# Learning-rate projection as 32-column blocks over token quarters, ahead of the value projections

## What is computed

```
XQ = rope(heads(xn @ q_w.T)); XK = rope(heads(xn @ k_w.T)); XV = heads(xn @ v_w.T)
ttt_lr = sigmoid(einsum('bnkc,hdc->bhnkd', Xc, lr_w) + lr_b)
eta = token_idx * ttt_lr / HD          # used in every step of the scan
out = scan(step, (W1, b1), chunks of (XQ, XK, XV, eta))
y = ln(out) @ o_w.T
```

## Time and profile before

| what | us |
|---|---|
| median of 3 runs | 676.73 (676.66 to 681.01) |
| the profiled execution | 677.36 |
| its span in the trace | 675.3 |
| what lies around the span | 2.06 |

### The profile page before, as it was taken

The page is one execution under the profiler, slowest core; times in us unless marked ns, Lnnn a source line. Parts: engine busy times, 40 slices in busy tenths (PEclk is TensorE's granted clock), DMA queues, the critical chain, the costliest instruction groups (busy, mean ns, idle before and its releaser), DMA issues. The chain is left out here.

```text
span 675.3 us, 30660 instructions
## 1 busy us (share of the span) xinstructions
PE 523.9 (78%) x12150; PEld 365.4 (54%) x12150; DVE 474.2 (70%) x1484; ACT 365.1 (54%) x1172; POOL 339.4 (50%) x595
## 2 busy tenths in 40 slices
PE   0399999997477777777777777777776499859997
PEld 0143333444466777766777677677775244445552
DVE  6456776753668888888888888888897267528331
ACT  0424443223556666666666766666665576544432
POOL 0368888775334544544555445455543656421223
PEclk9999999997555555555555555555555699969999
DMA  9101111113900000000000000000000700000113
GB/s 348 48 8 40 39 39 32 31 31 79 203 6 2 0 0 0 0 0 0 0 0 0 0 0 0 0 0 0 0 3 3 282 1 0 1 1 1 65 73 114
DMA packets 9849, 24.54 MB, mean 36 GB/s; under 512 B 1845, under 2 KB 2510, under 8 KB 9550
## 3 DMA queue, kind: packets, MB, share of 16 engines
q1 hardware_dynamic: 9806, 24.01, 11.5%
HBM read 11.42 MB, written 4.19 MB: 23 GB/s over the span
## 5 line engine op out<-in xcount | busy, mean ns | idle before, releaser
L762 PE MATMUL PS<-work 32*32 32x32 f32 x4064 | 84.5, 238 | 60.0 <-DVE work L911 52.7
L762 PEld LDWEIGHTS PS<-work 32*32 32x32 f32 x4064 | 80.4, 152 | 70.2 <-issue 66.7
L751 PE MATMUL PS<-work 64*32 64x64 f32 x2048 | 69.6, 310 | 24.1 <-ACT work L1002 20.5
L500 PE MATMUL PS<-X,work 128*128 (+3 forms) x160 | 72.4, 599 | 6.4 <-ACT X L640 6.3
L751 PEld LDWEIGHTS PS<-work 64*32 64x32 f32 x2048 | 55.7, 163 | 31.2 <-issue 29.8
L774 PE MATMUL PS<-work 32*64 32x32 f32 x2016 | 68.4, 292 | 1.1 <-issue 1.1
L966 POOL TENSOR_TENSOR work<-work 128x128 f32<-128x128 f32 x64 | 25.5, 399 | 80.7 <-DVE work L911 77.2
L774 PEld LDWEIGHTS PS<-work 32*64 32x64 f32 x2016 | 59.7, 216 | 5.3 <-issue 1.3
L958 POOL TENSOR_TENSOR work<-work,mask 128x256 f32<-128x256 f32 x64 | 46.7, 730 | 13.6 <-ACT work L1034 7.3
L942 POOL TENSOR_TENSOR work<-KP,cst 128x256 f32<-128x256 f32 x64 | 39.2, 612 | 26.5 <-DVE work L870 21.5
L500 PEld LDWEIGHTS PS<-X,work 128*128 128x128 f32 (+1 forms) x160 | 26.1, 171 | 47.7 <-issue 47.2
(11 more groups left out here) (145 smaller groups left out, 1301.2 us busy)
## 6 DMA issues: line engine op xcount, KB each, us to landing
X<-in_x SPq DMA_DIRECT2D x4, 1024.0 KB, 8.0
TK<-KP SPq DMA_DIRECT2D x64, 64.0 KB, 1.9
X<-QP SPq DMA_DIRECT2D x8, 512.0 KB, 9.0
TK<-in_x SPq DMA_DIRECT2D x4, 1024.0 KB, 8.9
out<-TK SPq DMA_DIRECT2D x16, 256.0 KB, 2.2
work<-in_rope SPq DMA_DIRECT2D x2, 512.0 KB, 9.7
cst<-in_consts SPq DMA_DIRECT2D x1, 289.0 KB, 4.8
work<-in_wk SPq DMA_DIRECT2D x1, 256.0 KB, 11.1
```

The costliest lines, as they stand in the source:

```text
L500: mm = nc.tensor.matmul(o, lhs(j), xt(i, j), start=(j == 0), stop=(j == J - 1))
L751: mm = nc.tensor.matmul(PS[HD * a:HD * a + HD, ZB[p], b * ZW:b * ZW + ZW], KT2[p][r:r + 64, k * B + b, :, :].rearrange("p e t -> p (e t)") ...
L762: mm = nc.tensor.matmul(PS[HD * a:HD * a + HD, bank, b * width:b * width + HD], AM[p][HD * a:HD * a + HD, b, part, :, :].rearrange("p e t ...
```

## The change

The rates are computed with 32 weight columns instead of 8 (24 are zeros, set by a memset on POOL; SP's load of wl waits for it). Four matmuls for each channel half take 128 tokens each and write them to the partitions 0-31, 32-63, 64-95 and 96-127 of bank 2, columns 0 to 127. They stand after the four rotary projections, ahead of the widening and the value projections. lr_out becomes a copy of 128 partitions x 128 columns, ahead of the two v_out; it goes to lrt for block 0 and to the first 128 columns of the block i-1 of X, which is done with. PE's hardware loop over the blocks becomes straight code for all of them, and ACT's body 0 is taken out of its loop. At the end there are eight 128 x 128 transposes into the banks 1 and 2 in place of the 32, and two sigmoids of 128 columns in place of one of 256.

```diff
--- before.py
+++ after.py
@@ -226,12 +226,13 @@
         sd = carve(P)
         kc, ksw = carve(2, BLK), carve(2, BLK)
         wkv = carve(J, 2 * C)
-        wl = carve(J, NH)
+        wl = carve(J, HD)
         sum_x, sum_sq = carve(BLK), carve(BLK)
         wvw = wsm
         lrt = sb("lrt", [P, 8 * B * NH])
         s_k0 = sem("s_k0")
         s_pick = sem("pick_rows")
+        s_wl0 = sem("wl_zero")
         s_w, s_rt, s_sp2 = sem("s_w"), sem("ropetab"), sem("spread_table")
 
         FIRST = CONST_AT["spread"][0]
@@ -246,7 +247,8 @@
             sp.dma_start(wkv[:, :, 0:C], wk).then_inc(s_w, 16)
             sp.dma_start(wkv[:, :, C:2 * C], wq).then_inc(s_w, 16)
             sp.dma_start(wvw[:, :, :], wv).then_inc(s_w, 16)
-            sp.dma_start(wl, wlr).then_inc(s_w, 16)
+            sp.wait_ge(s_wl0, 1)
+            sp.dma_start(wl[:, :, 0:NH], wlr).then_inc(s_w, 16)
             sp.dma_start(cosT, rope[:, 0, :]).then_inc(s_rt, 16)
             sp.dma_start(sinT, rope[:, 1, :]).then_inc(s_rt, 16)
             sp.dma_start(cst[:, FIRST:], consts[:, FIRST:]).then_inc(s_sp2, 16)
@@ -298,6 +300,7 @@
                 pool.memset(eps5, EPS_GN).then_inc(s_k0, 1)
                 pool.memset(eps6, EPS_IN).then_inc(s_k0, 1)
                 pool.memset(one, 1.0).then_inc(s_k0, 1)
+                pool.memset(wl, 0.0).then_inc(s_wl0, 1)
                 pool.memset(pick[:, :, :], 0.0).then_inc(s_pick, 1)
                 pool.wait_ge(s_pick, 1)
                 for g in range(4):
@@ -450,6 +453,12 @@
                 sem(n) for n in ("proj", "kc", "ksw", "ksin", "rope", "tt", "lr", "kperm", "ttf", "lr_tr", "sig",
                                  "lr_spread", "lr_h"))
             NPJ = 7
+
+            def rate_rows(i):
+
+                if isinstance(i, int) and i == 0:
+                    return lrt[:, 0:P]
+                return X[:, 0, ds((i - 1) * BLK, P)]
 
             @block.sync
             def _(sp):
@@ -478,26 +487,26 @@
                 def proj(i, m, first):
                     if m < 2 * J:
                         lhs = lambda j: wkv[:, j, m * P:(m + 1) * P]
-                    elif m < 3 * J:
+                    else:
                         lhs = lambda j: wvw[:, j, (m - 2 * J) * P:(m - 2 * J + 1) * P]
-                    else:
-                        lhs = lambda j: wl[:, j, :]
-                    if m == NPJ - 1:
-                        first_tile = value(pe, i * (2 * J) + 1)
-                        pe.wait_ge(s_w, 64)
-                        pe.wait_ge(s_ksw, first_tile)
-                        o = PS[0:NH, 2, :]
-                    else:
-                        o = PS[:, 2 + m, :]
-                        if not first:
-                            if m < 2 * J:
-                                pe.wait_ge(s_ksw, (i - 1) * (2 * J) + m + 1)
-                            else:
-                                pe.wait_ge(s_tt, (i - 1) * J + m - 2 * J + 1)
-                            if m == 0:
-                                pe.wait_ge(s_lr, i + 0)
+                    if not first:
+                        if m < 2 * J:
+                            pe.wait_ge(s_ksw, (i - 1) * (2 * J) + m + 1)
+                        else:
+                            pe.wait_ge(s_tt, (i - 1) * J + m - 2 * J + 1)
+                        if m == 0:
+                            pe.wait_ge(s_lr, i + 0)
                     for j in range(J):
-                        mm = nc.tensor.matmul(o, lhs(j), xt(i, j), start=(j == 0), stop=(j == J - 1))
+                        mm = nc.tensor.matmul(PS[:, 2 + m, :], lhs(j), xt(i, j), start=(j == 0), stop=(j == J - 1))
+                    mm.then_inc(s_proj, 1)
+
+                def rates(i):
+                    pe.wait_ge(s_ksw, value(pe, i * (2 * J) + 1))
+                    for j in range(J):
+                        for g in range(4):
+                            mm = nc.tensor.matmul(PS[HD * g:HD * g + HD, 2, 0:P], wl[:, j, :],
+                                                  xt(i, j)[:, g * P:(g + 1) * P], start=(j == 0),
+                                                  stop=(j == J - 1), skip_group_check=True)
                     mm.then_inc(s_proj, 1)
 
                 def body(i, first):
@@ -506,9 +515,12 @@
                     if has(i, 1):
                         pe_var(pe, i + 1, False)
                     pe.wait_ge(q1["xn"], i * J + J)
-                    for m in range(NPJ):
-                        if m == 2 * J and has(i, 1):
-                            pe_widen(pe, i + 1, False)
+                    for m in range(2 * J):
+                        proj(i, m, first)
+                    rates(i)
+                    if has(i, 1):
+                        pe_widen(pe, i + 1, False)
+                    for m in range(2 * J, 3 * J):
                         proj(i, m, first)
 
                 pe_mean(pe, 0, True)
@@ -516,21 +528,16 @@
                 pe_var(pe, 0, True)
                 pe_widen(pe, 0, True)
                 body(0, True)
-                with pe.Fori(1, NBLK - 2) as i:
+                for i in range(1, NBLK):
                     body(i, False)
-                body(NBLK - 2, False)
-                body(NBLK - 1, False)
 
                 pe.wait_ge(s_lr, NBLK)
                 pe.wait_ge(q1["xh"], NBLK * J)
-                for b in range(B):
-                    for s in range(8):
-                        tr = nc.tensor.transpose(PS[:, 1, (s * B + b) * NH:(s * B + b + 1) * NH],
-                                                 X[0:NH, 0, b * N + s * P:b * N + (s + 1) * P],
-                                                 ident[0:NH, 0:NH])
+                for i in range(NBLK):
+                    tr = nc.tensor.transpose(PS[:, 1 + i // 4, (i % 4) * P:(i % 4 + 1) * P], rate_rows(i), ident)
                 tr.then_inc(s_tr, 1)
 
-                pe.wait_ge(s_sig, 1)
+                pe.wait_ge(s_sig, 2)
                 pe.wait_ge(s_sp2, 16)
                 pe.wait_ge(q1["xc"], NBLK * J)
                 for n in range(8):
@@ -631,14 +638,14 @@
             @block.scalar
             def _(act):
                 def v_out(i, j):
-                    act.wait_ge(s_proj, i * NPJ + 2 * J + j + 1)
+                    act.wait_ge(s_proj, i * NPJ + 2 * J + j + 2)
                     nc.scalar.activation(TT[:, j, ds(i * BLK, BLK)], PS[:, 2 + 2 * J + j, :], ACT.Identity,
                                          scale=neg_g[:, j:j + 1], bias=bbg[:, j:j + 1]).then_inc(s_tt, 1)
 
                 def lr_out(i):
-                    act.wait_ge(s_proj, i * NPJ + NPJ)
-                    nc.scalar.activation(X[0:NH, 0, ds(i * BLK, BLK)], PS[0:NH, 2, :], ACT.Identity,
-                                         bias=pcol("lr_b", rows=NH)).then_inc(s_lr, 1)
+                    act.wait_ge(s_proj, i * NPJ + 2 * J + 1)
+                    nc.scalar.activation(rate_rows(i), PS[:, 2, 0:P], ACT.Identity, bias=pcol("lr_b")
+                                         ).then_inc(s_lr, 1)
 
                 def body(i):
                     if has(i, 1):
@@ -649,9 +656,9 @@
                         act_square(act, i + 2, False)
                     if has(i, 1):
                         act_affine(act, i + 1)
+                    lr_out(i)
                     for j in range(J):
                         v_out(i, j)
-                    lr_out(i)
 
                 act.wait_ge(s_sp, 2 * J)
                 act_a(act, 0)
@@ -661,12 +668,17 @@
                 act_sd(act, 0, True)
                 act_square(act, 1, False)
                 act_affine(act, 0)
-                with act.Fori(0, NBLK - 3) as i:
+                body(0)
+                with act.Fori(1, NBLK - 3) as i:
                     body(i)
                 for i in range(NBLK - 3, NBLK):
                     body(i)
                 act.wait_ge(s_tr, 1)
-                nc.scalar.activation(lrt[:, :], PS[:, 1, 0:8 * B * NH], ACT.Sigmoid).then_inc(s_sig, 1)
+                for k in range(2):
+                    nc.scalar.activation(
+                        lrt.rearrange("p (s b h) -> p b s h", s=8, b=B)[:, 2 * k:2 * k + 2, :, :],
+                        PS[:, 1 + k, :].rearrange("p (b s h) -> p b s h", b=2, s=8)[:, :, :, 0:NH], ACT.Sigmoid
+                    ).then_inc(s_sig, 1)
```

## The result

| | before | after |
|---|---|---|
| median of 8 runs each, us | 678.0 (676.66 to 681.5) | 671.45 (669.89 to 673.74) |
| profiled execution, us | 677.36 | 672.6 |
| span, us | 675.3 | 670.4 |

The ratio of the times is 0.9897, with a 95% interval of 0.9869 to 0.9924: 1.0% faster, 6.55 us by the medians. The forecast was 669.8 in a range of 666.0 to 674.5, with 0.50 for faster by over 1% and 0.47 for within 1%; the interval has 0.99 inside, so the runs don't decide between these two. The median lies 1.65 us above the forecast; the gain is 6.55 where 6.9 was forecast, and the rest of the distance is the kernel before, whose median over eight runs is 678.0 and not the 676.73 from which I started.

A forecast was written before the change was run, and what follows sets the result against it. The prediction took a ring of POOL, DVE and ACT, without PE, to bound the projections. Blocks gave 1.28 + 1.00 + 1.23 + 1.54 = 5.05 us, with the tail 6.9: 677.36 - 6.9 = 670.5, median 669.8, range 666.0 to 674.5.

The forecast's parts named there:

- The ring without PE: Projections: a closed chain of waits through POOL, DVE and ACT sets the 15.42 us from one token block to the next.
- lr_out, 0.32 a turn: Projections: ACT's smaller copy of the rates saves 0.32 us per block in four blocks, 1.28 us.
- The rates, 0.43 to 0.60 on PE: Projections: sixteen passes take 0.43 us, 0.60 with changes of shape, replacing 1.88; by itself this buys nothing in the middle.
- PE's earlier start: Projections: PE starts 1.64 us earlier against the ring; blocks 5, 6 and 7 gain 1.00, 1.23 and 1.54 us.
- The tail: After the last projection block, v_out to spread: the spread starts at 153.6 instead of 160.48, 6.9 us earlier.
- The straight code: PE's unrolled loop moves its instruction-fetch stop in the scan: taken as zero, between 3.38 us gained and 13.1 lost.
- PE as the bound: Rival 1, projections: PE binds, four turns give 5.3 us instead of 1.28, total 665.8 us; chance 0.10.
- the sizes wrong: Rival 2: column groups run serially (1.71 us), ACT's copy gets no shorter; some 3.7 us gained, 673 us; chance 0.20.
- the third: Rival 3, early scan: PE runs out of code until eight transfers finish, at worst 13.1 us lost, 682.9; chance 0.05.
- The Trainium skill's rule on instruction fetching: Instructions come in 16 KiB blocks, fetched ahead, mostly hidden; by it straight code costs nothing and 669.8 us stays.

The follow-up runs named there:

- the ring cut: Changed kernel with ACT's scale of a block (act_a) issued one block sooner, in ACT's idle time: 667.53 us, ratio 0.9794 against the kernel before.
- the place alone: Changed kernel with the old rates (8 columns, 512 tokens, large copy, 32 transposes) in the new place: 672.54 us, ratio 0.9888 against the kernel before.
- the hold-back: Eight transfers X<-QP let go one by one from the scan's ninth chunk: changed kernel 664.56 us (0.9767), kernel before 672.88 us (0.9887).
- The form alone: Changed kernel with rates and their copy put back last on PE and ACT, new shapes kept: 678.04 us, ratio 0.9986 against the kernel before.

## Why the prediction was right, point by point

- **The ring without PE bounds the turn.** Right, and shown by both signs: 0.86 us more on PE changes nothing, 1.7 more by a slow clock neither, 0.25 more on ACT lengthens each turn by 0.25, and with the ring cut at act_a the turn falls to POOL's 14.04 (14.09 follows from the prediction's 15.42 less POOL's 1.33).
- **lr_out, 0.32 a turn.** Right in the ordinary turn, 15.42 to 15.10, and by its size: in its new place with the old size (the place alone) it gives nothing in the turn. That POOL reaches block 4 1.33 us earlier, where 1.28 was forecast for four turns, is partly luck. By its product for the second key tile the four turns gave 0.36, 0.12, 0.33 and 0.33, 1.14 in all, since the second has the 0.2 of ACT described above; 0.19 were there before the first of them.
- **The rates, 0.43 to 0.60 on PE.** Right: 0.64 with the last pass's tail, 0.57 from start to start. It wasn't a term of the sum in the middle, and three times as much of it cost nothing.
- **PE's earlier start.** Right in size: 1.33 and 1.62 between the last blocks, 1.23 and 1.54 forecast. I had written about 1.6 us for PE's wait for lr_out; it is 0.96, and another 0.64 lies ahead of the variance, where PE waits for DVE's scale to have read bank 1. The sum was right, the place of a part wasn't, and no term of the time hung on it.
- **The tail.** The spread at 153.49, forecast 153.6. That the scan starts 6.97 us earlier is good to a few tenths: the two kernels with the hold-back, whose projections are the same code, have 6.7 between them.
- **The straight code.** Taken as zero with bounds of -3.38 and +13.1: -1.8 when done alone, at most +0.46 in the profile of after, where 0.4 remain with the stops gone. That zero was so near is luck: the stops to the 7th chunk are worth 8.1 us in the kernels before and after and 4.9 in the place alone. The reason that I gave, that what was asked for comes when the queues empty, holds by half: in the trace one block came at 170.2, with the transfers still running, and the next at 179.0, as they ended.
- **What I left out.** The forecast of the profiled execution was 670.5 and it took 672.6. Of the 2.1 us, 0.46 lie in the scan's first chunks, and 1.79 behind the scan, most of them in four passes that ran at the lower clock. No term of the sum stood for the clock. In the projections too it fell once, at no cost; with the hold-back, whose projections are the same code, it didn't fall.
- **The rivals.** PE as the bound would have given 665.8 and a turn of 14.1; the sizes wrong, 673 and 15.42. (Its own terms give 1.0 + 0.91 + 1.2 and a tail of 1.83 - 1.30 - 0.5, near 3.1 and not 3.7 us, so rather 673.6.) The turn of 15.10 decides against both. Of the third, the block of code that comes late is real, but it cost at most 0.5 us more than before and not 6.9.
- **The Trainium skill's rule on instruction fetching** (Runtime: NRT & Kernel Launch, section Instruction fetch mechanics: fetched ahead, mostly hidden) holds in the projections, where the straight code cost nothing (turn 15.41), and doesn't where eight transfers of 512 KB are on the queues: 8.1 us of stops came and went with them.

## What to carry to other kernels

Before counting on relief for the busiest engine, follow each wait of one turn back until the chain closes on itself; what the fullest engine does outside that chain was worth nothing here as long as it had room to wait, and a quarter of a microsecond on an engine that idles most of the time may count in full. A cheap way to be sure is to load each engine a little more and see whose load appears in the turn. Keep large transfers away from the first pass through new code, since instructions come over DMA too (the profile counts them as queue q8): that was worth 8.1 us in the scan's first chunks here, more than the 6.97 of the change itself.

## What the runs showed of the hardware

- **TensorE's clock can fall in the middle of a stage that looks full.** The form alone lost some 2.7 us of its projections to it in two of three profiles at hand (scan start 163.2 twice, with and without the hold-back, 160.3 once), with PE 1.11 us busy of the 3 us ahead of the first fall. The changed kernel lost the clock there in one of two profiles, with 1.83 us busy in both, and it cost that one nothing. The kernel with PE's load tripled in blocks 1 to 4 and the one with the ring cut, where PE waits 0.65 us in a turn, kept the full clock through the projections. The timed runs of the form alone, at 678, mostly have a mean granted clock of 0.711 where its first profile has 0.717; that they lost their time in the same way is likely by this, but no trace of them shows the place.
- **Instruction blocks wait behind data.** PE stood still for up to 5.2 us in the scan's first chunks and POOL once for 4.6 of its own, with DVE and ACT waiting for PE; of the 16 KB blocks of queue q8 one came from 158 to 178, three with the queues quiet.
- **A copy out of PSUM on ACT is paid by its columns far more than by its partitions:** 8 x 512 takes 0.57 us from start to start, 128 x 512 takes 0.66, and 128 x 128 takes 0.25: four times the elements of the first in less than half the time.
